# Gated delta rule layer on one core: Z1 ahead of the key sums, P0 and P1 behind the first two U1 products

## The reference

```python
mixed = jax.nn.silu(_causal_conv1d(hidden_states @ w_qkv, conv_w))
q, k, v = jnp.split(mixed, [KDIM, 2 * KDIM], axis=-1)
q, k = _l2norm(q), _l2norm(k)              # per head of 128
...
def step(St, inp):                         # 256 steps for each batch row and head
    St = St * jnp.exp(g_t)[..., None, None]
    delta = (v_t - jnp.einsum('bhk,bhkv->bhv', k_t, St)) * b_t[..., None]
    St = St + k_t[..., None] * delta[:, :, None, :]
    o = jnp.einsum('bhk,bhkv->bhv', q_t, St)
...
core = core * jax.lax.rsqrt(var + EPS) * norm_weight * jax.nn.silu(z)
return core.reshape(Bb, Ss, VDIM) @ w_out
```

## Time and profile before

| | |
|---|---|
| median of 3 runs | 1118.04 us (1117.95 to 1124.83) |
| span of the profiled execution | 1109.1 us |
| outside of the span (median less span) | 8.9 us |
| PE, DVE, ACT, POOL busy | 93%, 72%, 57%, 47% of the span |
| mean granted TensorE clock | 0.977 |

### The profile page before, as it was taken

One profiled execution on the slowest core, in us unless ns is written; L12 is line 12 of the kernel. 1 busy time (PEld: TensorE's weight loads), 2 busy tenths in 40 slices (PEclk: granted clock), 3 DMA queues, 4 the chain that ended last, 5 costly groups with the idle time before them and its releaser, 6 DMA issues.

```text
span 1109.1 us, 22258 instructions
## 1 busy us (share of the span) xinstructions
PE 1031.2 (93%) x8190; PEld 789.6 (71%) x8190; DVE 800.8 (72%) x1469; ACT 634.3 (57%) x1176; POOL 522.6 (47%) x1140
## 2 busy tenths in 40 slices
PE   4999999997789999999999999999999999996897
PEld 4886666655476877777777778686777777783776
DVE  4532243438769898988888898889898988897444
ACT  4421122316547677676767576777766675774453
POOL 3521000017865556473837474654738374645610
PEclk8999999999879999999999999999999999998999
DMA  9932110014342423324151434243341514332121
GB/s 328 397 142 77 43 48 30 20 65 150 55 134 37 124 45 117 60 101 109 53 122 56 106 74 126 38 124 47 115 96 66 122 54 107 74 97 39 27 47 48
DMA packets 183513, 103.16 MB, mean 93 GB/s; under 512 B 155632, under 2 KB 169584, under 8 KB 180080
## 3 DMA queue, kind: packets, MB, share of 16 engines
q1 hardware_dynamic: 181872, 97.55, 32.1%
q0 software_dynamic: 1536, 4.20, 1.2%
HBM read 79.77 MB, written 21.95 MB: 92 GB/s over the span
## 4 chain that ended last, share of the span: by engine, by line
PE 49%; DVE 14%; ACT 7%; issue 4%; POOL 2%; DMA 1%; SPq 0%; ACTq 0%; DVEq 0%
PE rg L1522 8%; DVE nm L1286 6%; PE rg L1505 5%; PE rg L1489 5%; PE pj L1382 4%; DVE shared_down_or_conv L1249 4%; PE pj L1383 4%; PE pj L1384 4%; PE rg L1497 3%; PE rg L1423 3%; PE rg L1506 2%; ACT vn L1221 2%; ACT sqk L1175 2%; PE rg L1477 2%; PE rg L1468 2%
## 5 line engine op out<-in xcount | busy, mean ns | idle before, releaser
L1088 POOL TENSOR_TENSOR rows<-rows,shared_down_or_conv 128x126 f32<-128x126 f32 (+22 forms) x496 | 189.6, 382 | 235.7 <-DMA shared_down_or_conv<-n_scratch 198.1
L1249 DVE SCALAR_TENSOR_TENSOR shared_down_or_conv<-pj,taps,shared_down_or_conv 128x510 f32<-128x510 f32 x372 | 275.1, 744 | 17.2 <-ACT shared_down_or_conv L1138 8.4
L1091 POOL TENSOR_TENSOR rows<-rows 128x126 f32<-128x126 f32 (+22 forms) x496 | 196.7, 397 | 38.9
L1382 PE MATMUL pj<-xhi,whi 128*128 128x512 f32 x376 | 165.3, 440 | 12.0 <-DVE shared_down_or_conv L1249 11.0
L1286 DVE SCALAR_TENSOR_TENSOR nm<-rg,wneg,hidden_or_decays 128x512 f32<-128x512 f32 (+1 forms) x256 | 139.2, 608 | 18.8 <-PE rg L1425 18.7
L1384 PE MATMUL pj<-xhi,wlo 128*128 128x512 f32 x376 | 150.8, 401 | 0.0
L1383 PE MATMUL pj<-xlo,whi 128*128 128x512 f32 x376 | 150.6, 401 | 0.0
L1138 ACT ACTIVATE shared_down_or_conv<-pj,taps 128x512 f32<-128x512 f32 x124 | 85.0, 687 | 89.8 <-PE pj L1384 87.7
L1522 PE MATMUL rg<-wo,gated 128*128 128x256 f32 x512 | 129.1, 387 | 0.1
L1382 PEld LDWEIGHTS pj<-xhi,whi 128*128 128x128 f32 x376 | 72.0, 192 | 53.7 <-issue 29.8
L1522 PEld LDWEIGHTS rg<-wo,gated 128*128 128x128 f32 x512 | 94.1, 191 | 14.7 <-issue 1.3
(11 more groups left out here) (216 smaller groups left out, 1986.2 us busy)
## 6 DMA issues: line engine op xcount, KB each, us to landing
hidden_or_decays<-eg_scratch SPq DMA_DIRECT2D x16, 1536.0 KB, 8.5
wraw<-w_heads SPq DMA_DIRECT2D x16, 776.0 KB, 4.4
w1a<-w_up SPq DMA_DIRECT2D x10, 1024.0 KB, 9.7
shared_down_or_conv<-n_scratch SPq DMA_DIRECT2D x32, 256.0 KB, 4.1
w2a<-w_down SPq DMA_DIRECT2D x8, 512.0 KB, 13.1
wo<-w_out SPq DMA_DIRECT2D x16, 256.0 KB, 2.6
n_scratch<-nm SPq DMA_DIRECT2D x64, 64.0 KB, 2.1
rt_scratch<-shared_down_or_conv SPq DMA_DIRECT2D x32, 128.0 KB, 2.3
```

Source lines behind the costliest of these rows:

```text
L1088: gp.tensor_tensor(tmp, rb[:, 0:r, t:t + 1].to_broadcast([P, r, w]), nb[:, t:t + 1, t + 1:].to_broadcast([P, r, w]), ALU.mult).then_inc(el ...
L1091: gp.tensor_tensor(rb[:, 0:r, t + 1:], rb[:, 0:r, t + 1:], tmp, ALU.add).then_inc(elim, 1)
L1249: v.scalar_tensor_tensor(out=y, in0=it.pbank[item][:, :, 0:S - s], scalar=taps[par][:, piece(j)[0], KS - 1 - s:KS - s], in1=y, op0=ALU.mul ...
L1382: te.matmul(bank, whi[par][w], xhi[:, k, cols], start=(k == 0), stop=False)
```

## The change

Two items move in PE's common order, one pair in ACT's. Nothing is added or taken out, DVE's order stays as it is, and so do the turns of the banks. The iterations 1 to 12 are affected.

```diff
-            ORDER = ("SO P4 Z0 SQ Z1 K0 K1 OUT0 Z2 P5 Z3 K2 OUT1 OUT2 P6 P7 LA1 K3 LA2 OUT3 OUT4 LB1 OUT5 LB2 P0 OUT6 "
-                     "U1_0 U1_1 N21_0 N21_1 P1 U2_0 P2 P3 U2_1 VT0 OUT7 O0 VT1 O1 O2 O3 VT2 VT3").split()
-            ORDER_A = ("SQ SO P4 E0 Z0 E1 Z1 P5 E2 Z2 W SK S4 LA1 E3 P6 LA2 Z3 S5 LB1 P7 S6 LB2 U1_0 P0 U1_1 S7 P1 S0 P2 "
+            ORDER = ("SO P4 Z0 Z1 SQ K0 K1 OUT0 Z2 P5 Z3 K2 OUT1 OUT2 P6 P7 LA1 K3 LA2 OUT3 OUT4 LB1 OUT5 LB2 OUT6 "
+                     "U1_0 U1_1 P0 P1 N21_0 N21_1 U2_0 P2 P3 U2_1 VT0 OUT7 O0 VT1 O1 O2 O3 VT2 VT3").split()
+            ORDER_A = ("SQ SO P4 E0 Z0 E1 Z1 P5 E2 Z2 W SK S4 LA1 E3 P6 LA2 Z3 S5 LB1 P7 S6 LB2 U1_0 U1_1 P0 S7 P1 S0 P2 "
```

## The result

The changed kernel takes 1135.16 us in the median of 6 runs (1132.43 to 1135.93), the kernel before 1119.78 us in 6 runs (1117.59 to 1125.41). The ratio is 1.011, 95% interval [1.0083, 1.0136]. It is slower by about 1%; the forecast was 1121.6 us in a range of 1115.5 to 1127.5. One execution among the later runs, of before_d2_behind_k1 in its second session, took 2214.7 us where the other seven took 1113.96 to 1122.86, and is left out of its ratio.

A forecast was written before the change was run, and what follows sets the result against it. Two floors bound it: PE's order (50.14 us) and the K3-LA1 loop (50.85). With +0.1 and +0.4 on PE and 0.2 to 0.8 on the loop, +0.3 in 12 iterations gave 1121.6 us, range 1115.5 to 1127.5.

The forecast's parts named there:

- The floors: Per iteration: PE's own order costs 50.14 us, the closed loop K3 to LA1 to K3 50.85; the larger bounds.
- The key sums 1.1 us later: Head of the iteration: behind Z1, the key sums come 1.0 to 1.2 us later, and DVE's work slides by 1.1.
- Z2: PE at Z2 waits for P4's convolution on DVE, now ending near 601.8; the gain is gone, with a loss of 0.1.
- give PE no place to win it back: After Z2: the end of P5's convolution and K1's `nm`, on which P7 and OUT2 wait, let PE regain nothing.
- the +0.1 for the head: Z1 ahead of the key sums: PE's order +0.1 us an iteration, bounds -0.5 and +0.4.
- K3 in the loop: From LA1 to the end of the next K3's `nm`: 4.92 us becomes 5.1 to 5.7, DVE being later.
- The collision: Rival, chance 0.13: D2's scan meets GpSimd's copy L1094, DVE 2.2 us late at K3; 51.7 us an iteration, time 1126.5.
- the sum's own 51.15: PE's 50.65 plus an LA1 wait of 0.5 us makes a 51.15 us iteration; with jitter 51.3.
- The rule on the shared ports: DVE's two-input scan contends with GpSimd's SBUF reads; whichever came first holds the ports throughout, so the copy blocks the scan.
- U1_0: PE at U1_0 waits for ACT's copies of LB2 with OUT6 alone in the gap: 0.4 us, bounds 0 and 0.5.
- Convolutions in time for P3 and U2_0: P0's convolution makes P3 with 0.1 us to spare; the rival, P3 or U2_0 late, had 0.08, some +10 us.
- 8.9 us outside of the span: Whole run: the median was taken as 8.9 us more than the profiled span, 1112.7 becoming 1121.6.

The follow-up runs named there:

- before_d2_behind_k1: The kernel before with DVE's scan D2 behind K1's `nm` and ACT's E2 behind Z2 and W: 50.41 us an iteration, ratio 0.996 to before; again, 0.993.
- z1_alone: The kernel before with only Z1 moved ahead of the key sums, P0, P1 and ACT's order as before: 51.46 us an iteration, ratio 1.005 to before.

## Why the prediction was wrong

The direction was right (+3.6 us forecast, slower), the size was not.

- **The floors.** Two floors side by side, 50.14 and 50.85 us, is confirmed from the other side: shortening the loop, with PE's order untouched, gained 0.6 us an iteration in two runs. PE's new order was forecast at 50.65; with the scan out of the way its shortest iteration takes 50.69. That what PE saves is waited away was right too.
- **The key sums 1.1 us later.** Measured against the square: 821.65 - 817.36 = 4.29 us, against 597.10 - 593.86 = 3.24. Right, 1.05.
- **Z2.** Visible waits of 0.17 to 0.34 us in 6 of 12; the gain at the key sums is used up here. Right.
- **"give PE no place to win it back".** This is the step that failed. The prediction puts K1's `nm` at nothing within the +0.1 for the head and names OUT2 as what waits for it; by the turns of the banks OUT1, one item earlier, waits for its first half. It never set the 1.1 us of lateness against OUT1's distance, which was 0.63 to 0.97 us and is 0.14 to 0.15 now. And it took D2 at its 1.26 us. With a scan of 1.6 to 2.2 us OUT1 waits 0.43 to 1.00 (six of twelve), with a short one 0.10 to 0.12. Iterations in which LA1 shows no idle time took at least 51.35 us, 1.2 over the 50.14 of before, where +0.5 was forecast. The head also cost more than +0.1 beside that: z1_alone's iterations, less what PE idles at OUT1 and at the join, take 50.6 us in the median where those of before take 50.2.
- **K3 in the loop.** Forecast 5.1 to 5.7 us from LA1 to the end of K3's `nm`, measured 5.36 to 5.38 where LA1 waited less than 0.3 us and 4.92 where it waited 0.44 or more. Right in size where LA1 hardly waits; the 0.2 us of lateness forecast for a wait of 0.63 didn't show.
- **The choice between the rivals.** The collision was a rival with 0.13, "as near as can be". It was the common case: 6 and 9 of 12. Its price, 51.7 us an iteration and +8 us, was the one measured (51.72, 51.81), but not by its path, so the agreement is in part luck: it had DVE 2.2 us late at K3 and LA1 waiting 1.05. In the six iterations with a long scan PE waits at OUT1 first, LA1 doesn't wait, and K3's `nm` ends 5.36 to 5.38 us behind LA1. Luck too is that the two kernels with D2 moved came out at 51.15 and 51.16, the sum's own 51.15 ahead of its jitter: the sum has DVE late at K3 and the elimination at 29.09 us, and neither kernel has both.
- **The rule on the shared ports.** Two iterations bear it out to within 0.2 us. In iteration 3 the copy started first, at 465.04 for 1.13 us, to 466.17; D2 began at 465.44, and 466.17 plus 1.26 is 467.43 against a measured end of 467.31. In iteration 10 the scan came 0.05 us ahead of the copy, at 827.25; the copy was 0.4 longer, and the second scan then waited for the copy's end at 828.86 and closed at 829.41, 0.55 later, where half a pair takes 0.63. So each engine stood for about as long as the other's instruction still ran. That is what the Trainium skill, SBUF — State Buffer, section Who interferes with whom, says; a scan with two SBUF inputs against a GpSimd copy falls under it. The rows of iteration 3:

```profile
465.04 1.13 POOL L1094 COPY shared_down_or_conv<-rows 128x512 f32<-128x512 f32 x1
...
465.44 1.87 DVE L1258 TENSOR_TENSOR_SCAN hidden_or_decays<-hidden_or_decays,start 128x256 f32<-128x256 f32 x2
...
469.95 0.45 PE L1522 MATMUL rg<-wo,gated 128*128 128x256 f32 x1 [0.71 <-DVE nm L1286]
```

- **U1_0.** Forecast 0.4 us. OUT6 now starts at 484.00 and U1_0 at 485.33, 1.33 us apart where it was 0.86: 0.47. The profile calls only 0.20 of it idle. Right:

```profile
484.00 0.48 PE L1522 MATMUL rg<-wo,gated 128*128 128x256 f32 x1
...
485.33 0.38 PE L1489 MATMUL rg<-vn,rf 128*128 128x128 f32 x1 [0.20 <-ACT rf L1207]
```

- **Convolutions in time for P3 and U2_0.** No wait shows there in the twelve. Right, but barely: in iteration 10 P0's convolution ends at 856.15 and P3 starts at 856.38, and U2_0 starts 0.05 us behind the addition of N21_0 in all twelve, so that it had nothing left to spare.
- **8.9 us outside of the span.** Wrong. In the changed kernel that was 1134.73 - 1132.9 = 1.8 us. A first profile of 1109.1 us under a median of 1118 meant that the profiled execution was one without the standstill near 50 us. It left the forecast's difference intact, but it made 23.8 us between two profiles look like an effect.

## What to carry to other kernels

When an order is moved so that an engine idles longer, look at what its later instructions will now run beside, not only at who waits for them: here a lateness of 1 us used up the 0.6 to 1.0 us by which OUT1 had stood clear of DVE, and meeting one GpSimd copy then cost TensorE up to 1.00 us. So for each item that waits for the late engine, write down by how much it stands clear today, the short distances that no list of waits shows included. A wait that sits in a closed loop through four engines is shortened in the loop; moving the 1.26 us scan that interfered with GpSimd was worth 0.6 us an iteration, while the two moves on TensorE lost 0.4 and 0.25. Try a repair on the old order too: this one gave the same 0.6 us with and without the change, so it hid the loss and did not explain it. And hold a span against the median: where they differ by far more than in other runs (8.9 us here, against 1.8), divide the trace by marks before and behind the change, and profile the unchanged kernel a second time before reading a difference of two profiles.

## What the runs showed of the hardware

Two engines kept each other from their work in both directions: VectorE's scan pair went from 1.26 to as much as 2.16 us beside a GpSimd copy, the copy from 1.16 to 1.56. No wait shows this in the profile: the instruction's own duration grows. Near 50 us of the program VectorE stood for 4 to 8 us, and ScalarE beside it for 3 to 6, in some sessions and not in others, in the same code; its cause was not looked for.
